# Products with V in four column groups instead of three, their lots at other slots, and a packed buffer for the small probabilities

## The chip, the cores and the metric

The kernel runs on one core of a Trainium2 chip. The metric is the device time of one execution in microseconds (us), the median of several runs. TensorE (PE) multiplies matrices, VectorE (DVE) and ScalarE (ACT) work element by element, GpSimd (POOL) and SyncE (SP) do small sums and issue transfers. PSUM is the memory into which TensorE writes, in banks of 128 partitions x 512 fp32.

## The reference, cut to what matters

32 images of 192 channels x 1024 tokens go through a channel attention (8 heads), then a token attention with a layer norm ahead, then a feed-forward part. Only the token attention is touched:

```
q = (x @ Wq).reshape(B, T, H, d)          # T = 1024, H = 6, d = 32
k, v = ...                                # the same with Wk, Wv
att = jnp.einsum('bqhd,bkhd->bhqk', q, k) * scale
att = jnp.where(causal, att, -jnp.inf)
att = jax.nn.softmax(att, axis=-1)
out = jnp.einsum('bhqk,bkhd->bqhd', att, v)
t = t + out.reshape(B, T, C)
```

Of the mask follows that query tile qt (128 queries, qt from 0 to 7) needs the keys of tiles 0 to qt alone.

## The kernel before

Five groups of six images each go through attention, and then through the feed-forward part of the group; two images are left and go through attention alone at the end. While the attention of one image runs, the "front" of the next image runs between its instructions: channel attention, layer norm, and the projections that make Q, K and V. The last image has no front beside it.

**Units and slots.** A unit is one head and one query tile: 48 per image. They are numbered n, alternate between a small tile (0 to 3) and a large one (4 to 7), and each has its slot. In slot n every engine does, in an order written out by hand:

- PE: the scores of unit n (L676, and the mask L678), once the exponential of unit n-2 has left that half of `S`; the transposes of the probabilities of unit n-3 (L690) into the two banks `PT`, up to four 128-column blocks a bank, a "chunk"; then, in some slots, a lot of products with V (L710); in some slots the transposes back of a finished batch (L719, "back" below); then a step of the next image's front (`SLOTS` gives the slot of each: xt0 to xt3, g0 to g1, wg0, wg1, na, rb, u, mt, t0 to t3, z0 to z3, qk0 to qk5, v0 to v3).
- DVE: the maximum of unit n (L1213), the copy of a large unit's first chunk to SBUF (L382), the adding of a batch to the tokens (L1199, L1201, L1207), then front work (layer norm: L1076, L1080, L1084, L1089; L1148 behind the qk steps).
- ACT: in one slot of a batch the copy of `OUT` (L925), the copy of a small unit's chunk (L928), the exponential of unit n (L936), the copy of a large unit's second chunk (L940), then front work.

Small units are turned in odd slots, large ones in even slots.

**Lots.** A lot is the product with V for three heads and one query tile. Each of its matmuls has 32 stationary columns of V and 128 moving columns, and the three heads write to partitions 0, 32 and 64 of `OUT`: three column groups of TensorE. For each key tile j the lot issues one matmul per head; this is a "step" below, and since an fp32 matmul is two instructions here, a step is six instructions. Units go in blocks of six (three heads x a small and a large tile), so an image has 16 lots and 72 steps. The small lot of block i stands in slot 6i+8, the large one in 6i+11. Four lots make a batch; ACT copies `OUT` in slot 12j+18, PE turns it back in slot 12j+19 into a `PT` bank, DVE scales and adds it.

Within an image the lots stand in slots 2, 5, 8, 11, ... 44, 47, with 3, 5, 2, 8, 4, 6, 1, 7 steps and then the same again; backs stand in slots 7, 19, 31 and 43.

**Buffers.** Turned probabilities lie in `PTS`: a ring of four per kind of unit, 512 columns each for small units and 1024 for large ones. Before it overwrites an entry, a copy waits for the lot that read it (`pv_made`). `stacked[0]` and `stacked[1]` tell that the transfers that lay out Q and K of heads 0 to 2 and 3 to 5 have landed (16 transfers per image, SP, L420).

Of the kernel before, what the change touches and what calls it, by code (L numbers as in the profile page):

```python
# [18 lines left out]
F32 = mybir.dt.float32  # L19
F16 = mybir.dt.float16  # L20
BF16 = mybir.dt.bfloat16
ALU = mybir.AluOpType
# [37 lines left out]
RING = 4  # L60
STACKS = 8 * 16
# [5 lines left out]

def qtile(n):
    return TILES[n // 6 % 4][n % 2]


def triple_of(n):
    return 2 * (n // 6) + n % 2


def unit_of(k, hh):
    return 6 * (k // 2) + k % 2 + 2 * hh


def last_slot(images):  # L80
    return 12 * (NBI * images - 1) + BACK_AT


def triples_at(images, slot):

    return [k for k in range(KI * images) if 6 * (k // 2) + PV_AT[k % 2] == slot]


def batches_at(images, slot, at):

    return [j for j in range(NBI * images) if 12 * j + at == slot]

# [9 lines left out]


def sum_col(n):

    k = triple_of(n)
    return 3 * (BATCH * (k // BATCH % SUMS) + place(k)) + n % 6 // 2

# [13 lines left out]
CHUNKS = {images: transposed(images) for images in (2, GROUP)}  # L122
PT_IMG = len(CHUNKS[2]) // 4
assert all(len(c) == 2 * PT_IMG * images for images, c in CHUNKS.items())

# [36 lines left out]
def hybrid_kernel(nc, x, wa, wb, wv, wpt, bp, temp, w3, w1, b1, w2, b2, out):  # L162
# [5 lines left out]
    with ctx:  # L168
# [3 lines left out]
        def sem(name):  # L172
# [37 lines left out]
        NK = sb("NK", [CH, 4])  # L210
        RD = sb("RD", [CH, 2, CH])
        ATT = RD
        MT = sb("MT", [CH + 1, 2, C])
# [3 lines left out]
        PROD = hi_z[0:CH + 1, :].bitcast(F32)[:, 0:4 * C].rearrange("p (a b) -> p a b", a=2)  # L217
        T0 = sb("T0", [P, 2, TT, C])
# [14 lines left out]
        T1H = T1[:, :, :, :].rearrange("p b (h t) c -> p b h (t c)", h=2)  # L233
        work = sb("work", [P, 9216])

        PS = [work[:, 0:1024].rearrange("p (a b) -> p a b", a=2), work[:, 1024:3072].rearrange("p (a b) -> p a b", a=2)]
        PTS = [work[:, 3072:5120].rearrange("p (a b) -> p a b", a=RING),
               work[:, 5120:9216].rearrange("p (a b) -> p a b", a=RING)]

# [3 lines left out]
        OT = work[:, 4096:4096 + 4 * 4 * C].rearrange("p (s n) -> p s n", s=4)  # L243
        oT = sb("oT", [CH, BATCH * P])
        rowsum = sb("rowsum", [P, 3 * BATCH * SUMS])
# [4 lines left out]
        rsums = sb("rsums", [P, 3 * BATCH])  # L250
        gm1 = sb("gm1", [P, GS, MH])
# [123 lines left out]
        def pt_copy(eng, copy, g, images, i):  # L375

            _, _, m, c0, k = CHUNKS[images][i]
            eng.wait_ge(pt_full[i % 2], after(g, 0, PT_IMG, i // 2 + 1))
            if m >= 2 * RING:

                eng.wait_ge(pv_made, after(g, 0, KI, triple_of(m - 2 * RING) + 1))
            copy(PTS[m % 2][:, m // 2 % RING, P * c0:P * (c0 + k)], PT[i % 2][:, 0:P * k]).then_inc(pt_free[i % 2], 1)  # L382

# [162 lines left out]
        def _(pe):  # L546
# [111 lines left out]
            for name in SLOTS:  # L658
                if name == "qk0":
                    pe.wait_ge(w3_ready, 1)  # L660
                front_part(name, 0, 0)

            def attention(g, images, fronts):
                for n in range(last_slot(images) + 1):
                    if n < UNITS * images:
                        u, h, qt = n // UNITS, 3 * (n % UNITS // 24) + n % 6 // 2, qtile(n)
# [13 lines left out]
                    for i, (_, kind, m, c0, k) in chunks_at(images, n):  # L680
# [4 lines left out]
                        if kind == "p":  # L685
                            if i >= 2:

                                pe.wait_ge(pt_free[i % 2], after(g, 0, PT_IMG, i // 2))
# [4 lines left out]
                    for k in triples_at(images, n):  # L693
                        u, grp, qt = k // KI, k % KI // 8, qtile(unit_of(k, 0))
                        done = [i for i, c in enumerate(CHUNKS[images]) if c[1] == "p" and c[2] <= unit_of(k, 2)]
                        for b in range(2):

                            pe.wait_ge(pt_free[b], after(g, 0, PT_IMG, max(i for i in done if i % 2 == b) // 2 + 1))
                        if k % KI == 0:

                            for step in STEPS[-2:]:
                                wait_freed(pe, g, u, step)
                        if k and k % BATCH == 0:

                            pe.wait_ge(oT_made, after(g, 0, NBI, k // BATCH))
                        o = P * place(k)
                        for j in range(qt + 1):
                            for hh in range(3):
                                h = 3 * grp + hh
                                last = mm(OUT[32 * hh:32 * hh + 32, o:o + P],  # L710
                                          V[u % 2][:, j, D * h:D * h + D], PTS[k % 2][:, unit_of(k, hh) // 2 % RING, P * j:P * j + P],
                                          start=(j == 0), stop=(j == qt), tile_position=(0, 32 * hh))
                        last.then_inc(pv_made, 1)
                    for i, (_, kind, j, _, _) in chunks_at(images, n):
                        if kind == "o":
                            pe.wait_ge(pt_free[i % 2], after(g, 0, PT_IMG, i // 2))
# [126 lines left out]
        def _(act):  # L843
# [74 lines left out]
            def attention(g, images, fronts):  # L918
                for n in range(last_slot(images) + 1):
                    for j in batches_at(images, n, OT_AT):  # L920
                        act.wait_ge(pv_made, after(g, 0, KI, BATCH * (j + 1)))
                        if j >= 1:

                            act.wait_ge(t1_step, after(g, 0, 3 * NBI, 3 * (j - 1) + 2))
                        A(oT[:, :], OUT[0:CH, :], ACT.Copy).then_inc(oT_made, 1)  # L925
                    for i, c in chunks_at(images, n):
                        if by_act(i, c) and small(c):
                            pt_copy(act, lambda o, x: A(o, x, ACT.Copy), g, images, i)  # L928
                    if n < UNITS * images:

                        act.wait_ge(max_made, after(g, 0, UNITS, n + 1))
                        if n >= 4:
                            i = max(i for i, c in enumerate(CHUNKS[images]) if c[1] == "p" and c[2] == n - 4)
                            act.wait_ge(pt_full[i % 2], after(g, 0, PT_IMG, i // 2 + 1))
                        w = P * (qtile(n) + 1)
# [69 lines left out]
        def _(dve):  # L1005
# [185 lines left out]
            def add_to_t1(g, i, j):  # L1191

                base = after(g, 0, 3 * NBI, 3 * j)
                dve.wait_ge(pt_full[i % 2], after(g, 0, PT_IMG, i // 2 + 1))
                n = 3 * BATCH
                u, grp, qts = j // NBI, j % NBI // 2, batch_tiles(j)
                ts, cols = slice(qts[0], qts[-1] + 1, 2), slice(CH * grp, CH * grp + CH)
# [3 lines left out]
                v.tensor_tensor(t1.rearrange("p t (h d) -> p t h d", h=3),  # L1201
                                PT[i % 2][:, 0:BATCH * CH].rearrange("p (t h d) -> p t h d", t=BATCH, h=3),
                                rsums[:, :].rearrange("p (t h) -> p t h", t=BATCH).unsqueeze(3).broadcast_to(
                                    [P, BATCH, 3, D]), ALU.mult).then_inc(t1_step, 1)
                dve.wait_ge(t1_step, base + 2)
# [185 lines left out]
```

## Time and profile before

| | |
|---|---|
| median of 3 runs | 4539.35 us (4538.74 to 4539.68) |
| profiled execution | 4540.19 us, its span 4538.4 us |
| PE busy | 4010.0 us (88%) |
| DVE busy | 3043.9 us (67%) |
| ACT busy | 2975.3 us (66%) |
| granted TensorE clock, mean | 0.977 |

The busy time of an engine is the union of its instructions' durations. Share of the span and bound are two things: an engine can be busy 88% of the time and yet set the pace in one stretch and wait in another. So the rows further on go by stretches of one image. A timeline row has the start, the time from the first start to the last end of the instructions merged in it, and in brackets the idle time of the engine ahead of it with what ended it.

### The profile page before, as it was taken

Reading aid. Unit: us, or ns where it says so; the run is one execution under the profiler, and the core shown is the slowest. Engines: PE = TensorE matmul, PEld = TensorE weight load, DVE = VectorE, ACT = ScalarE, POOL = GpSimd, SP = SyncE. Lnnn points to the kernel's source line nnn. Section 1 sums busy time; section 2 is a strip of 40 time slices with the busy share of each in tenths; the row PEclk is TensorE's granted clock in tenths of the full one; section 3 lists DMA queues with packets and bytes.
Section 4 is the critical chain, followed back from the end, with each engine's and each line's share of the span. In section 5 each row is a group of like instructions: output and inputs, shape, how many; then the busy total and the mean of one; then the engine's idle time right before and its main releaser. Section 6 shows DMA issues by size and latency. Waiting matters only on the chain.

```text
span 4538.4 us, 114718 instructions
## 1 busy us (share of the span) xinstructions
PE 4010.0 (88%) x39240; PEld 2939.7 (65%) x39240; DVE 3043.9 (67%) x5559; ACT 2975.3 (66%) x6669; POOL 363.7 (8%) x374
## 2 busy tenths in 40 slices
PE   6999988879999888999998879999888999898887
PEld 4767665667777646777665667777646777665665
DVE  5666666766666667666766766666666666766765
ACT  3666666657776655666676667776655676676666
POOL 1000002000000110000002000000110000002000
PEclk7999999999999999999999999999999999999999
DMA  2111111011221101111111011211101111111011
GB/s 72 37 37 36 43 36 29 1 50 36 54 47 36 36 0 43 36 37 36 43 36 29 1 50 38 57 42 36 36 0 43 37 36 41 39 36 29 1 43 43
DMA packets 48640, 161.00 MB, mean 35 GB/s; under 512 B 12420, under 2 KB 12934, under 8 KB 48006
## 3 DMA queue, kind: packets, MB, share of 16 engines
q1 hardware_dynamic: 48134, 154.39, 14.2%
q8 instruction: 300, 4.92, 0.5%
q14 instruction: 206, 1.69, 0.1%
HBM read 28.52 MB, written 25.17 MB: 12 GB/s over the span
## 4 chain that ended last, share of the span: by engine, by line
PE 63%; DVE 14%; issue 13%; ACT 6%; POOL 2%; DVEq 1%; DMA 1%; ACTq 1%; SPq 0%; POOLq 0%
PE PT L690 10%; PE OUT L710 10%; PE S L676 6%; DVE nmax L1213 5%; PE PT L808 5%; PE S L735 5%; PE S L634 3%; PE FR L634 3%; PE FR L578 2%; PE S L779 2%; ACT work L936 2%; DVE work L382 2%; DVE XT L1084 2%; PE FR L641 1%; PE S L641 1%
## 5 line engine op out<-in xcount | busy, mean ns | idle before, releaser
L1213 DVE TENSOR_REDUCE nmax<-S 128x1 f32<-128x256 f32 (+7 forms) x1536 | 1146.1, 753 | 937.0 <-PE S L678 927.0
L936 ACT ACTIVATE work<-S,nmax 128x256 f32<-128x256 f32 (+7 forms) x1536 | 1137.7, 742 | 613.9 <-DVE nmax L1213 594.8
L690 PE MATMUL PT<-ident,work 128*128 128x128 f32 x6912 | 1076.7, 280 | 93.2 <-DVE work L382 54.5
L690 PEld LDWEIGHTS PT<-ident,work 128*128 128x128 f32 x6912 | 748.2, 142 | 260.0 <-ACT work L928 54.3
L382 DVE COPY work<-PT 128x512 f32<-128x512 f32 x768 | 524.1, 682 | 45.0 <-PE PT L690 37.8
L928 ACT ACTIVATE work<-PT 128x256 f32<-128x256 f32 (+3 forms) x768 | 338.1, 440 | 153.6 <-PE PT L690 146.4
L676 PE MATMUL S<-KS,QS 128*128 128x512 f16 (+3 forms) x1152 | 323.5, 335 | 111.4 <-ACT work L936 76.9
L676 PE MATMUL S<-odd 128*128 128x512 f16 (+3 forms) x1152 | 315.5, 328 | 71.7 <-ACT work L936 68.0
L678 PE MATMUL S<-causal,identb 128*128 128x128 bf16 x1536 | 339.2, 221 | 0.0
L940 ACT ACTIVATE work<-PT 128x512 f32<-128x512 f32 (+3 forms) x768 | 332.4, 433 | 1.4 <-PE PT L690 1.4
L936 ACT ACTIVATION_READ_ACCUMULATOR work<-S,nmax 128x1 f32 x1536 | 304.6, 198 | 0.0
L735 PE MATMUL S<-odd,W1b 128*128 (+1 forms) x1080 | 259.7, 393 | 50.0 <-ACT work L979 41.7
L710 PE MATMUL OUT<-work,V 128*32 128x128 f32 x6912 | 303.1, 275 | 0.0
L710 PE MATMUL OUT<-work,odd 128*32 128x128 f32 x6912 | 302.6, 275 | 0.0
L1247 DVE TENSOR_REDUCE gm<-S 128x1024 f32 (+1 forms) x180 | 220.0, 1222 | 118.7 <-PE S L779 117.7
L779 PE MATMUL S<-odd,W1b 128*128 (+1 forms) x1080 | 291.8, 379 | 0.0
L979 ACT ACTIVATE work<-S,sc 128x512 f32<-128x512 f32 x360 | 255.0, 781 | 51.2 <-PE S L735 50.7
L710 PEld LDWEIGHTS OUT<-work,V 128*32 128x32 f32 x6912 | 234.3, 110 | 40.9 <-issue 32.3
L710 PEld LDWEIGHTS OUT<-work,odd 128*32 128x32 f32 x6912 | 234.5, 109 | 40.2 <-issue 30.7
L808 PE MATMUL PT<-W2b,work 128*128 128x192 f16 x2880 | 247.5, 246 | 8.8 <-DVE odd L1300 8.8
L808 PEld LDWEIGHTS PT<-W2b,work 128*128 128x128 f16 x2880 | 239.0, 98 | 22.9 <-DVE odd L1300 9.9
L1292 DVE SCALAR_TENSOR_TENSOR work<-work 128x1024 f16<-128x1024 f32 x180 | 218.3, 1224 | 30.2 <-ACT work L986 26.1
(208 smaller groups left out, 6113.6 us busy)
## 6 DMA issues: line engine op xcount, KB each, us to landing
X<-in_x SPq DMA_DIRECT2D x32, 768.0 KB, 5.3
odd<-hi_z SPq DMA_DIRECT2D x128, 192.0 KB, 4.2
odd<-odd SPq DMA_DIRECT2D x128, 192.0 KB, 4.3
out_y<-work SPq DMA_DIRECT2D x64, 384.0 KB, 4.0
QS<-hi_z SPq DMA_DIRECT2D x64, 192.0 KB, 3.9
QS<-odd SPq DMA_DIRECT2D x64, 192.0 KB, 4.1
KS<-hi_z SPq DMA_DIRECT2D x64, 192.0 KB, 4.6
KS<-odd SPq DMA_DIRECT2D x64, 192.0 KB, 4.7
```

Source lines behind the costliest of these rows:

```text
L382: copy(PTS[m % 2][:, m // 2 % RING, P * c0:P * (c0 + k)], PT[i % 2][:, 0:P * k]).then_inc(pt_free[i % 2], 1)
L676: mm(S[:, n % 2, c0:min(w, c0 + 512)], q, KS[u % 2][:, h, c0:min(w, c0 + 512)], start=True, stop=c0 + 512 < w)
L678: mm(S[:, n % 2, w - P:w], identb[:, :], causal[:, :], start=False, stop=True).then_inc(scores_full, 1)
L690: last = tr(bank[:, P * (j - c0):P * (j - c0) + P], PS[m % 2][:, m // 2 % 2, P * j:P * j + P], ident[:, :])
L710: last = mm(OUT[32 * hh:32 * hh + 32, o:o + P], V[u % 2][:, j, D * h:D * h + D], PTS[k % 2][:, unit_of(k, hh) // 2 % RING, P * j:P * j + P ...
L735: last = mm(bank, W1b[:, j, P * (i % 6):P * (i % 6) + P], rhs[:, j, :], start=(j == 0), stop=(j == 2))
L779: last = mm(bank, W1b[:, j, P * m:P * m + P], Z2[:, b, hf, j, :], start=False, stop=(j == 2))
L808: last = mm(PT[tp % 2][:, C * t:C * t + C], HS[:, hf, part, m, o:o + P], W2b[:, m, :], start=(m == 0 and part == 0), stop=(m == MH - 1 and ...
L928: pt_copy(act, lambda o, x: A(o, x, ACT.Copy), g, images, i)
L936: A(PS[n % 2][:, n // 2 % 2, 0:w], S[:, n % 2, 0:w], ACT.Exp, bias=nmax[:, n % MAXES:n % MAXES + 1], accum_out=rowsum[:, sum_col(n):sum_co ...
L940: pt_copy(act, lambda o, x: A(o, x, ACT.Copy), g, images, i)
L1213: v.tensor_reduce(nmax[:, n % MAXES:n % MAXES + 1], S[:, n % 2, 0:P * (qtile(n) + 1)], AX.X, ALU.max, negate=True).then_inc(max_made, 1)
```

## The change

- Units go in blocks of eight. In blocks 0 to 3 of an image these are heads 0 to 3 x (a small and a large tile); in blocks 4 and 5 they are heads 4 and 5 with two small and two large tiles each: (0, 1) and (6, 7), then (2, 3) and (4, 5).
- A lot takes four units and four column groups (`OUT` partitions 0, 32, 64, 96). An image has 12 lots. In blocks 4 and 5 a lot's two tiles differ by one, so its last step has two matmuls instead of four.
- The large lot of block i stands in slot 8i+11, the small one in slot 8i+14. Within an image: slots 3, 6, 11, 14, 19, 22, 27, 30, 35, 38, 43, 46, with 6, 4, 8, 2, 6, 4, 7, 1, 5, 3, 8, 2 steps.
- A batch is still four lots, so there are three per image, with 128 partitions and 512 columns: copied in slot 16j+23, turned back in 16j+24 (slots 8, 24, 40 of an image; the copies in 7, 23, 39).
- Turned small probabilities are packed by their width into 2304 columns, odd blocks from the end downward; turned large ones have four entries of 1024 columns. What a copy overwrites is given by `overwritten`.
- Head 3 is needed from unit 6 of an image on, so `stacked[1]` is waited for there and not at unit 24.
- `RD`, `ATT` and `MT` move into unused columns of `hi_z`, which makes room.

```
-KI = UNITS // 3
+KI = UNITS // 4
 TILES = [(1, 7), (3, 5), (0, 6), (2, 4)]
+PAIRS = [((0, 1), (6, 7)), ((2, 3), (4, 5))]
-PV_AT = (8, 11)
+PV_AT = (14, 11)
-OT_AT, BACK_AT = 18, 19
-RING = 4
+OT_AT, BACK_AT = 23, 24
+SMALL = 2304
+def head_and_tile(n):
+    block, at, large = n % UNITS // 8, n % 8 // 2, n % 2
+    if block < 4:
+        return at, TILES[block][large]
+    return 4 + at % 2, PAIRS[block - 4][large][at // 2]
+def lots_until(k):
+    return k if k % 2 else k + 2
+def turned_at(m):
+    k, hh = quad_of(m), m % 8 // 2
+    if m % 2:
+        return 1024 * hh
+    widths = [P * (qtile(unit_of(k, i)) + 1) for i in range(hh + 1)]
+    return SMALL - sum(widths) if k // 2 % 2 else sum(widths[:hh])
+def overwritten(m):
+    k = quad_of(m)
+    return k - 2 if m % 2 or m % 8 >= 4 else k - 4
...
-            if m >= 2 * RING:
-                eng.wait_ge(pv_made, after(g, 0, KI, triple_of(m - 2 * RING) + 1))
+            if overwritten(m) >= 0:
+                eng.wait_ge(pv_made, after(g, 0, KI, lots_until(overwritten(m))))
...
+                for j in range(max(qtile(m) for m in units) + 1):
+                    for hh, m in enumerate(units):
+                        h, qt = head_and_tile(m)
+                        if j <= qt:
+                            last = mm(OUT[32 * hh:32 * hh + 32, o:o + P], V[u % 2][:, j, D * h:D * h + D],
+                                      PTS[k % 2][:, turned_at(m) + P * j:turned_at(m) + P * j + P],
+                                      start=(j == 0), stop=(j == qt), tile_position=(0, 32 * hh))
...
-                        if n % 24 == 0:
-                            pe.wait_ge(stacked[n % UNITS // 24], after(g, u, STACKS, STACKS))
+                        if n % UNITS in (0, 6):
+                            pe.wait_ge(stacked[h // 3], after(g, u, STACKS, STACKS))
...
-                                last = tr(PT[i % 2][:, CH * q:CH * q + CH], oT[:, P * q:P * q + P],
-                                          ident[0:CH, 0:CH])
+                                last = tr(PT[i % 2][:, P * q:P * q + P], oT[:, P * q:P * q + P], ident[:, :])
```

## Rows read from the trace of the kernel before

**Rows 1.** The page: engines' busy time, and its chain that ended last.

```profile
PE 4010.0 (88%) x39240; PEld 2939.7 (65%) x39240; DVE 3043.9 (67%) x5559; ACT 2975.3 (66%) x6669; POOL 363.7 (8%) x374
...
PE 63%; DVE 14%; issue 13%; ACT 6%; POOL 2%; DVEq 1%; DMA 1%; ACTq 1%; SPq 0%; POOLq 0%
```

**Rows 2.** Busy time by window: one whole image, then the image without a front.

```profile
core 0: us, PE busy (x) PEld busy (x) DVE busy (x) ACT busy (x) POOL busy (x), PEclk, DMA share, GB/s
...
1147.20:1250.00 102.80, 94.69 (x1021) 72.54 (x1020) 69.12 (x132) 72.12 (x179) 6.03 (x5) 1.00 0.17 40
...
4440.10:4517.20 77.10, 64.15 (x740) 45.59 (x738) 54.06 (x84) 55.40 (x145) 0.00 (x0) 1.00 0.05 12
```

**Rows 3.** Busy time by window: slots 0-11, 12-23, 24-34, 35-47 of that image.

```profile
1146.80:1173.90 27.10, 26.45 (x283) 21.06 (x281) 15.47 (x23) 18.18 (x45) 0.00 (x0) 1.00 0.14 33
1173.90:1199.80 25.90, 22.98 (x242) 18.88 (x241) 17.08 (x42) 16.22 (x45) 1.00 (x1) 1.00 0.01 2
1199.80:1220.00 20.20, 16.29 (x170) 11.26 (x167) 18.40 (x38) 14.74 (x35) 5.03 (x4) 1.00 0.16 40
1220.00:1249.60 29.60, 28.99 (x332) 21.32 (x332) 18.17 (x28) 22.98 (x55) 0.00 (x0) 1.00 0.37 80
```

**Rows 4.** PE's timeline, slots 35 and 43 to 44: lots of 8 and of 1 step, a back.

```profile
1220.41 0.60 PE L690 MATMUL PT<-ident,work 128*128 128x128 f32 x4
1220.95 1.95 PE L710 MATMUL OUT<-work,V 128*32 128x128 f32 x48
1222.83 0.39 PE L634 MATMUL FR<-zt,W3h 128*128 128x512 f16 x1
...
1241.09 0.50 PE L719 MATMUL PT<-ident,oT 96*128 96x96 f32 x4
1241.42 0.25 PE L641 MATMUL FR<-W3h,zt 128*128 128x192 f16 x1
...
1243.49 0.42 PE L710 MATMUL OUT<-work,V 128*32 128x128 f32 x6
1243.85 0.26 PE L641 MATMUL S<-W3h,zt 128*128 128x192 f16 x1
```

**Rows 5.** PE's timeline, slots 2 to 5.

```profile
1150.01 0.86 PE L710 MATMUL OUT<-work,odd 128*32 128x128 f32 x18
...
1154.41 0.60 PE L676 MATMUL S<-KS,QS 128*128 128x512 f16 x2 [0.65 <-ACT work L936]
```

**Rows 6.** Timeline, slots 17 to 19: the wait of front step u, the back.

```profile
1181.26 0.55 PE L676 MATMUL S<-KS,QS 128*128 128x512 f16 x2 [0.99 <-ACT work L936]
...
1181.91 1.51 PE L710 MATMUL OUT<-work,V 128*32 128x128 f32 x36
...
1185.78 0.89 PE L610 MATMUL FR<-WPT,RD 96*96 96x192 f32 x4 [1.26 <-DVE RD L1129]
...
1187.40 0.54 PE L719 MATMUL PT<-ident,oT 96*128 96x96 f32 x4 [0.23 <-ACT work L940]
```

**Rows 7.** DVE's timeline, slots 24 to 31: only first rows and the batch.

```profile
1200.18 0.42 DVE L1213 TENSOR_REDUCE nmax<-S 128x1 f32<-128x256 f32 x1 [2.23 <-PE S L678]
1200.71 0.69 DVE L382 COPY work<-PT 128x512 f32<-128x512 f32 x1
1201.32 1.21 DVE L1213 TENSOR_REDUCE nmax<-S 128x1 f32<-128x1024 f32 x1
...
1214.46 0.23 DVE L1199 RECIPROCAL rsums<-rowsum 128x12 f32<-128x12 f32 x1 [0.56 <-PE PT L719]
1214.72 0.56 DVE L1201 TENSOR_TENSOR T<-PT,rsums 128x384 f32<-128x384 f32 x1
1215.44 0.56 DVE L1207 TENSOR_TENSOR T<-T 128x384 f32<-128x384 f32 x1 [0.16 <-DVE T L1201]
```

**Rows 8.** PE's timeline at the end of a group's attention.

```profile
718.67 2.11 PE L710 MATMUL OUT<-work,odd 128*32 128x128 f32 x48
```

**Rows 9.** SP's timeline: the last stacking transfers of the image.

```profile
1249.61 2.06 SPq L420 DMA_DIRECT2D odd<-odd  x2
```

More of the change, by code:

```diff
@@ L65, with quad_of, quads_at @@
          284: "next_stats1", 285: "next_aggregate", 286: "turn0", 287: "turn1", 288: "turn2", 289: "turn3"}
-def qtile(n):
-    return TILES[n // 6 % 4][n % 2]
-def triple_of(n):
-    return 2 * (n // 6) + n % 2
+def head_and_tile(n):
[3 more added lines that the diff above has]
+    return 4 + at % 2, PAIRS[block - 4][large][at // 2]
+def qtile(n):
+    return head_and_tile(n)[1]
+def quad_of(n):
+    return 2 * (n // 8) + n % 2
+def lots_until(k):
+    return k if k % 2 else k + 2
 def unit_of(k, hh):
-    return 6 * (k // 2) + k % 2 + 2 * hh
+    return 8 * (k // 2) + k % 2 + 2 * hh
 def last_slot(images):
-    return 12 * (NBI * images - 1) + BACK_AT
-def triples_at(images, slot):
-    return [k for k in range(KI * images) if 6 * (k // 2) + PV_AT[k % 2] == slot]
+    return 16 * (NBI * images - 1) + BACK_AT
+def quads_at(images, slot):
+    return [k for k in range(KI * images) if 8 * (k // 2) + PV_AT[k % 2] == slot]
 def batches_at(images, slot, at):
-    return [j for j in range(NBI * images) if 12 * j + at == slot]
+    return [j for j in range(NBI * images) if 16 * j + at == slot]
 def batch_tiles(j):
@@ L122 @@
 CHUNKS = {images: transposed(images) for images in (2, GROUP)}
-PT_IMG = len(CHUNKS[2]) // 4
-assert all(len(c) == 2 * PT_IMG * images for images, c in CHUNKS.items())
+PT_GROUP = len(CHUNKS[GROUP]) // 2
+assert len(CHUNKS[GROUP]) == 2 * PT_GROUP
 STEPS = ["xt0", "xt1", "xt2", "xt3", "g0", "g1", "wg0", "wg1", "na", "rb", "u", "mt", "t0", "t1", "t2", "t3",
@@ L661, in _, with times_v @@
                 front_part(name, 0, 0)
+            def times_v(g, images, k):
+                u, units = k // KI, [unit_of(k, hh) for hh in range(4)]
+                done = [i for i, c in enumerate(CHUNKS[images]) if c[1] == "p" and c[2] <= units[3]]
+                for b in range(2):
+                    pe.wait_ge(pt_free[b], g * PT_GROUP + (max(i for i in done if i % 2 == b) // 2 + 1))
+                if k % KI == 1:
+                    for step in STEPS[-2:]:
+                        wait_freed(pe, g, u, step)
+                if k > BATCH and k % BATCH == 1:
+                    pe.wait_ge(oT_made, after(g, 0, NBI, k // BATCH))
+                o = P * place(k)
+                for j in range(max(qtile(m) for m in units) + 1):
[5 more added lines that the diff above has]
+                                      start=(j == 0), stop=(j == qt), tile_position=(0, 32 * hh))
+                last.then_inc(pv_made, 1)
             def attention(g, images, fronts):
@@ L686, in attention @@
                             if i >= 2:
[L688 removed]
+                                pe.wait_ge(pt_free[i % 2], g * PT_GROUP + i // 2)
                             for j in range(c0, c0 + k):
@@ L692, in attention @@
                             last.then_inc(pt_full[i % 2], 1)
[L693 to L713, printed above, removed]
+                    for k in quads_at(images, n):
+                        times_v(g, images, k)
                     for i, (_, kind, j, _, _) in chunks_at(images, n):
                         if kind == "o":
-                            pe.wait_ge(pt_free[i % 2], after(g, 0, PT_IMG, i // 2))
+                            pe.wait_ge(pt_free[i % 2], g * PT_GROUP + i // 2)
                             pe.wait_ge(oT_made, after(g, 0, NBI, j + 1))
                             for q in range(BATCH):
-                                last = tr(PT[i % 2][:, CH * q:CH * q + CH], oT[:, P * q:P * q + P],
-                                          ident[0:CH, 0:CH])
+                                last = tr(PT[i % 2][:, P * q:P * q + P], oT[:, P * q:P * q + P], ident[:, :])
                             last.then_inc(pt_full[i % 2], 1)
@@ L1193, in add_to_t1 @@
                 base = after(g, 0, 3 * NBI, 3 * j)
[L1194 to L1197, printed above, removed]
+                dve.wait_ge(pt_full[i % 2], g * PT_GROUP + (i // 2 + 1))
+                n = 4 * BATCH
+                u, qts = j // NBI, batch_tiles(j)
+                if j % NBI < 2:
+                    ts, cols, nt, nh = slice(qts[0], qts[-1] + 1, 2), slice(0, 4 * D), 4, 4
+                else:
+                    ts, cols, nt, nh = slice(0, TT), slice(4 * D, C), TT, 2
                 t1 = T1[:, u, ts, cols]
```

43 lines of the change are left out of this document (22 added, 21 removed).

## The prediction

> **What bounds the kernel now.** I read the page first. TensorE is busy 88% of the span, VectorE 67%, ScalarE 66%, and 63% of the chain that ended last is PE's [rows 1]. That says where to look, not what a PE microsecond is worth, because attention is a loop across three engines: scores, maximum, exponential, and the scores two units later. So I next took windows. An image with a front takes 102.8 us with PE busy 94.69; the image without one takes 77.1 us with PE busy 64.15 [rows 2]. The front adds 30.5 us of PE work and 25.7 us of time, so PE is nearly the bound, but with 8.1 us of idle time that is not spread evenly.
>
> Windows by stretch of slots show where it is [rows 3]. In slots 0 to 11 PE is busy 26.45 of 27.10 us and in slots 35 to 47 28.99 of 29.60: what leaves PE there leaves the time. In slots 12 to 23 it idles 2.9 us. In slots 24 to 34 it is busy only 16.29 of 20.20 us, while DVE, which does the layer norm there, is busy 18.40: DVE sets that stretch. The change has to be priced stretch by stretch.
>
> **Price of a lot.** A lot of 8 steps (48 instructions) occupies PE from its start to the start of the next work for 1222.83 - 1220.95 = 1.88 us, a lot of one step for 0.36 us [rows 4]. A step is then (1.88 - 0.36) / 7 = 0.217 us, whatever the number of heads in it as far as three go, and a lot costs 0.14 us more behind it. Four transposes ahead of the long lot last 0.54 us, of which about 0.44 is theirs (0.109 each, the pitch of half a step), so 0.10 is the change into the lot [rows 4]. I take 0.24 us per lot beside its steps.
>
> The step has three heads in three column groups before and four in four after. No row shows four side by side. If the fourth fits, a step stays 0.217 us. If it does not, the bound is one third more, 0.29 us. I take 0.217: with three heads 1.52 us for 42 instructions are 36 ns for each, while the transposes ahead, which also stream 128 fp32 columns but use all columns of the array, come at about three times that (0.54 us for four, the change included). So the three groups do run side by side, at the pitch of one. The skill's page "TensorE: Matmul & The Clock Gate", Part 3 on packing small matmuls, gives 2.38x for three column tiles and 3.07x for four row tiles. By that ratio four heads would take 1.034 times the step of three, an estimate of 0.4 us more per image on 56 steps; no run here shows it yet, and the sum below does without it.
>
> **PE's work, per image.** Steps fall from 72 to 56: 16 x 0.217 = 3.47 us. Lots fall from 16 to 12: 4 x 0.24 = 0.96 us. A back costs 1241.42 - 1241.09 = 0.33 us at 96 rows [rows 4]; at 128 a third more, 0.44; four at 0.33 against three at 0.44 is nothing. The ceiling is thus 4.43 us per image. Now by stretch, with what hides or exposes each.
>
> **Slots 0 to 11.** 18 steps before and after, one lot fewer: -0.24. One back before and after: +0.11. The lot in slot 2 is in a part where the exponential sets the pace; without it PE waits there for the same exponential and gains little, while the lot now in slot 3 fills the 0.65 us that PE idled ahead of slot 5 [rows 5]. About +0.05. The back now stands in an even slot, behind a large unit's two chunks; its bank is the one of the first chunk, which DVE frees only after its maximum: in slot 24 that copy ends 1201.40 - 1199.82 = 1.6 us into the slot [rows 7], and PE has turned its eight blocks by about 1.2. A wait of 0 to 0.65 us, taken as 0.4. Sum +0.3 us.
>
> **Slots 12 to 23.** 18 steps become 12 (-1.30), four lots three (-0.24), and the back leaves (-0.33): -1.87. But the lot in slot 17 runs while front step u waits for the channel softmax (DVE and ACT); PE idles 1.26 us more after it [rows 6]. That chain hangs on the scores of unit 17, not on the lot, so without the lot PE waits its 36 instructions' time longer: +1.54. The 0.23 us of waiting ahead of the back [rows 6] goes. Sum -0.56 us.
>
> **Slots 24 to 34.** Three lots become two, but PE is not the bound, so that is worth nothing by itself. DVE adds one batch in the stretch before (slot 31) and one after (slot 24). Before, DVE idled 0.56 us for the transposes and worked 1.35 us [rows 7]. After, the tensors have 512 columns instead of 384, an estimate of 1.6 us, and stand between the maximum of unit 24 and that of unit 25: maximum 25 started 1.5 us into slot 24 and would start at about 3.9, 2.4 us later, and the layer norm is queued behind it; the exponential of unit 25 and the scores of unit 27 wait for it. At slot 31 1.35 + 0.56 = 1.9 us come back. In sum +0.4 if DVE has no slack; -1.1 if the removal at slot 31 relieves PE and ACT too and the delay at slot 24 is absorbed by the idle time that DVE has ahead of it (2.23 us [rows 7]). The middle, -0.35.
>
> **Slots 35 to 47.** 26 steps become 18 (-1.74), five lots four (-0.24), the back +0.11, its wait in slot 40 +0.4. With the long lot gone from slot 47, PE reaches the next image's scores before the exponential of unit 47 has ended: +0.35, an estimate. Sum -1.1 us.
>
> **Other parts.** A large lot now waits for chunks turned one slot earlier (slot 8i+10, copied by ACT behind the exponential), three slots before. Where a front step lies between them that is hidden; in slots 3 and 27 it may cost up to 0.5 us each, inside the bounds above. The small lot stands five slots behind its last transposes and waits for nothing. The packed buffer is overwritten only after lots that PE has already issued: nothing. `stacked[1]` is now needed 18 units sooner; the last transfers are issued by 1251.67 [rows 9], slot 6 starts about 11 us after 1249.61, so with a few us to land it is in time. Moving `MT` and its like costs no instruction.
>
> **End of a group.** The last two lots run there back to back, 8 steps in 2.11 us [rows 8]; after, they have 10 and the long one, which waits for the last copies, comes first: +1.0 us, at five groups and the end, +6 us.
>
> **Sum.** 0.3 - 0.56 - 0.35 - 1.1 = -1.7 us per image; 31 images have a front: -53 us. The image without one is paced by the three-engine loop: 0. With the +6: -47 us on the profiled 4540.2 us, 4493 us; the median lies 0.8 us below the profiled run, so 4492 us.
>
> **Rivals.**
> - *PE's whole saving shows* (chance 0.15). The waits merely shift. For it: PE is 92% busy. Against it: the 18.40 us of DVE [rows 3] and the 1.26 us [rows 6]. 31 x 4.43 = 137 us: 4402 us.
> - *It evens out* (0.12). Stretch two gains nothing as its waits grow by all that leaves, stretch three takes +0.4, the two bank waits are 0.65: +0.55 + 0 + 0.4 - 0.85 = +0.1 per image, 31 x 0.1 + 6 us, 4548 us.
> - *DVE's batch at slot 24 is not recovered* (0.13), the one on the other side. If the 2.4 us by which maximum 25 slips reach the end of the stretch, because slots 31 to 34 are set by ACT's copies and not by the batch that left, stretch three costs +2.3 instead of -0.35: 31 x 2.65 = 82 us more, 4574 us. It turns the sign once it costs 47 / 31 = 1.5 us per image more than in my sum. Against it: PE and DVE both lose work at slot 31.
> - *The fourth group does not fit* (0.05). A step of 0.29 us: 40 of 56 steps lie on the path, 31 x 40 x 0.073 = 91 us more, 4583 us. The row's 36 ns per instruction speaks against it.
> The forecast holds 0.55, with its own range 4450 to 4525.
>
> **How the numbers follow.** Within 0.2% is 4530 to 4548, about what a measurement can tell from no change. Faster takes the forecast and the first rival, 0.70; the even case gives 0.13 with the edges of its neighbours, slower 0.17. The range that leaves out 2 in 10 cuts most of the slower rivals and the far end of the first: 4422 to 4550 us.
>
> **What would show it.** Per step 0.217 us with 8 instructions; windows of one image with PE busy about 90.3 us and a length near 101; PE waiting longer ahead of front step u; a wait for DVE's copy ahead of the backs in slots 8, 24 and 40; maximum 25 late by 2 us. The prediction is wrong if a step grows, if large lots wait for ACT's second chunk in most blocks, or if slots 24 to 34 get longer.

## The result, and the profile after

The changed kernel takes 4732.4 us (4726.0 to 4738.9, 4 runs) against 4539.5 us before, a ratio of 1.043 [1.041, 1.044]: 193 us slower, where 47 us faster was forecast with a range up to 4550.

The page of the kernel after, engines' busy time:

```profile
PE 3993.5 (84%) x39057; PEld 2924.3 (62%) x39112; DVE 3070.5 (65%) x5463; ACT 2941.6 (62%) x6637; POOL 362.8 (8%) x374
```

TensorE's busy time fell by only 16.5 us [rows 1]; four fewer lots and 16 fewer steps per image should take 31 x 4.43 = 137 us from it, and the image without a front another 4. So something else on TensorE got longer. The granted clock tells what: its mean is 0.949 after and 0.977 before. The clock has two levels, 2.4 and 1.2 GHz, so the half level held for (1 - 0.949) x 2 x 4729 = 482 us after and 209 us before.

Busy time by window after, the same image and the same stretches as in [rows 3]: slots 0 to 11, 12 to 23, 24 to 34, 35 to 47. The column ahead of the last two is the granted clock:

```profile
1193.40:1221.90 28.50, 26.86 (x312) 21.68 (x313) 16.50 (x24) 19.92 (x48) 0.00 (x0) 1.00 0.17 39
1221.90:1248.90 27.00, 23.30 (x228) 18.65 (x226) 16.68 (x39) 15.76 (x44) 1.00 (x1) 0.94 0.01 2
1248.90:1272.80 23.90, 16.72 (x168) 12.15 (x167) 17.66 (x38) 13.44 (x36) 5.01 (x4) 0.86 0.14 34
1272.80:1303.50 30.70, 28.18 (x314) 20.00 (x315) 19.28 (x28) 21.95 (x53) 0.00 (x0) 1.00 0.31 71
```

Against [rows 3] all four are longer: +1.4, +1.1, +3.7 and +1.1 us, together 110.1 us for 102.8. The two stretches in the middle are no longer at full clock; before, in this image, all four were. The image shown is one of the longer ones. Over 20 images (the second to the fifth of each group of six) the mean is 109.5 us for 103.1, and the four stretches take 1.3, 0.9, 3.0 and 1.1 us more; a table at the end of the experiments has these means for every run. The half clock of the two middle stretches is in all 31 images that have a front.

TensorE's timeline after, slots 11, then 18 and 19:

```profile
1217.88 1.96 PE L711 MATMUL OUT<-work,V 128*32 128x128 f32 x64
1219.76 1.52 PE L625 MATMUL FR<-ones,hi_z 97*96 97x1 f32 x16
...
1229.81 1.18 PE L743 MATMUL PT<-ident,work 128*128 128x128 f32 x6
1233.68 0.89 PE L640 MATMUL FR<-WPT,hi_z 96*96 96x192 f32 x4 [2.70 <-DVE hi_z L1162]
...
1235.21 2.79 PE L711 MATMUL OUT<-work,V 128*32 128x128 f32 x48
1237.93 1.67 PE L645 MATMUL S<-zt,WV 96*97 96x192 f32 x8
```

Two things are to be read here. The lot of 8 steps with four heads, 64 instructions, occupies TensorE for 1219.76 - 1217.88 = 1.88 us, to the hundredth what the lot of 8 steps with three heads took [rows 4]. The fourth column group is free. And the lot of six steps in slot 19, 48 instructions, takes 2.72 us to the next start, where 6 x 0.217 + 0.14 = 1.44 us are its price at full clock. Ahead of it TensorE had idled for 2.70 us at front step u. The idle time itself was in the sum (1.26 us before, 1.54 more); what it did to the clock was not.

Windows of TensorE after: the wait in slot 18, slot 19, slot 27.

```profile
1229.70:1233.60 3.90, 1.15 (x10) 0.68 (x7) 1.93 (x6) 2.41 (x7) 0.00 (x0) 1.00 0.01 2
1234.40:1239.40 5.00, 5.00 (x62) 4.00 (x60) 1.11 (x2) 2.06 (x5) 0.00 (x0) 0.66 0.01 3
1254.80:1260.40 5.60, 4.48 (x63) 3.25 (x64) 3.43 (x12) 2.32 (x6) 1.84 (x2) 0.54 0.00 0
```

In slot 19 TensorE is busy all of the time at a mean clock of 0.66. In slot 27 it is 0.54. Why TensorE came to wait ahead of slot 27 stands in two timelines after, slots 24 to 27. VectorE:

```profile
1249.74 0.68 DVE L412 COPY work<-PT 128x512 f32<-128x512 f32 x1
1251.24 0.25 DVE L1235 RECIPROCAL rsums<-rowsum 128x16 f32<-128x16 f32 x1 [0.82 <-PE PT L753]
1251.53 0.69 DVE L1237 TENSOR_TENSOR T<-PT,rsums 128x512 f32<-128x512 f32 x1
1252.37 0.69 DVE L1243 TENSOR_TENSOR T<-T 128x512 f32<-128x512 f32 x1 [0.15 <-DVE T L1237]
1252.98 0.82 DVE L1249 TENSOR_REDUCE nmax<-S 128x1 f32<-128x640 f32 x1
```

TensorE:

```profile
1250.55 0.65 PE L753 MATMUL PT<-ident,oT 128*128 128x128 f32 x4 [0.55 <-DVE work L412]
...
1254.77 0.44 PE L729 MATMUL S<-KS,QS 128*128 128x512 f16 x2 [1.40 <-ACT work L969]
...
1256.39 0.88 PE L743 MATMUL PT<-ident,work 128*128 128x128 f32 x3 [1.12 <-ACT work L969]
1257.20 3.21 PE L711 MATMUL OUT<-work,V 128*32 128x128 f32 x56
```

The batch of slot 24 waits for the copy of the large unit's first chunk (0.55 us on TensorE), then for the back (0.82 us on VectorE), then takes 1.7 us; only then comes the maximum of unit 25 (L1249, at 1252.98), 4.1 us into slot 24. Before it was 1.5 us [rows 7]. The exponential and with it the scores of unit 27 come late, TensorE idles 1.40 and 1.12 us, and the long lot runs at half clock: 3.15 us to the next start for 7 x 0.217 + 0.14 = 1.66.

In slot 40 the back waits in the same way, and a little later front step v0:

```profile
1287.87 0.65 PE L753 MATMUL PT<-ident,oT 128*128 128x128 f32 x4 [0.82 <-DVE work L412]
...
1291.15 0.26 PE L671 MATMUL FR<-W3h,zt 128*128 128x192 f16 x1 [0.79 <-DVEq L1185]
```

### The profile page after: what moved, and what is told of

Same layout as the page of the kernel before. It is cut to its first block, busy times and chain, and to the rows that moved or that the text cites. A ratio compares the mean times of both kernels' runs of the same rounds, so it can differ in the third digit from the quotient of the medians.

```text
span 4729.1 us, 114023 instructions
## 1 busy us (share of the span) xinstructions
PE 3993.5 (84%) x39057; PEld 2924.3 (62%) x39112; DVE 3070.5 (65%) x5463; ACT 2941.6 (62%) x6637; POOL 362.8 (8%) x374
## 4 chain that ended last, share of the span: by engine, by line
PE 60%; DVE 14%; issue 14%; ACT 7%; POOL 2%; DMA 1%; DVEq 1%; ACTq 1%; SPq 1%; POOLq 0%
PE OUT L711 10%; PE PT L743 10%; PE S L729 6%; PE PT L841 5%; PE S L768 4%; DVE nmax L1249 4%; DVE work L412 2%; ACT work L969 2%; PE S L812 2%; PE FR L608 2%; PE S L664 2%; PE FR L664 2%; PE FR L671 1%; PE PT L753 1%; PE S L731 1%
## 5 line engine op out<-in xcount | busy, mean ns | idle before, releaser
L1249 DVE TENSOR_REDUCE nmax<-S 128x1 f32<-128x256 f32 (+7 forms) x1536 | 1146.0, 753 | 964.3 <-PE S L731 932.1
L743 PE MATMUL PT<-ident,work 128*128 128x128 f32 x6912 | 1096.4, 284 | 140.2 <-DVE work L412 50.2
L743 PEld LDWEIGHTS PT<-ident,work 128*128 128x128 f32 x6912 | 769.0, 145 | 298.9 <-ACT work L961 59.8
L961 ACT ACTIVATE work<-PT 128x256 f32<-128x256 f32 (+3 forms) x768 | 339.2, 442 | 157.6 <-PE PT L743 148.6
L711 PE MATMUL OUT<-work,V 128*32 128x128 f32 x6912 | 271.1, 304 | 12.5 <-ACT work L973 12.5
L711 PE MATMUL OUT<-work,odd 128*32 128x128 f32 x6912 | 254.8, 292 | 14.5 <-ACT work L973 14.5
L711 PEld LDWEIGHTS OUT<-work,V 128*32 128x32 f32 x6912 | 211.3, 122 | 51.0 <-issue 30.9
L731 PEld LDWEIGHTS S<-causal,identb 128*128 128x128 bf16 x1536 | 154.2, 100 | 128.8 <-issue 21.0
```

The source lines that it names most:

```text
L711: last = mm(OUT[32 * hh:32 * hh + 32, o:o + P], V[u % 2][:, j, D * h:D * h + D], PTS[k % 2][:, turned_at(m) + P * j:turned_at(m) + P * j + P],
L1249: v.tensor_reduce(nmax[:, n % MAXES:n % MAXES + 1], S[:, n % 2, 0:P * (qtile(n) + 1)], AX.X, ALU.max, negate=True).then_inc(max_made, 1)
```

## The experiments

Two causes were to be told apart: theory C (the clock falls after TensorE's longer waits, and that is time lost) and theory D (the batch stands in the wrong slots for VectorE, and the clock only follows where TensorE waits anyway). Unless it says otherwise, each kernel is the changed kernel with the edit shown. "Image" is the length of the four stretches of one image in its profile; the kernel before has 27.1, 25.9, 20.2, 29.6 us there, the changed one 28.5, 27.0, 23.9, 30.7. The ratio behind each time is to the kernel before, run alongside.

**e1, matmuls in the waits.** Their results are not used; all other work is unchanged.

```
+                    for _ in range(7):       # front step u, ahead of its wait
+                        mm(FR[0:CH, 0:C], WPT[:, 0, 0:CH], WPT[:, 1, :], start=True, stop=True)
                     pe.wait_ge(xsoft, after(g, u, XSOFT, XSOFT))
...
+                    if n % UNITS in {26: 4, 30: 4} and n // UNITS < fronts:
+                        keep_busy(g, n // UNITS + 1, {26: 4, 30: 4}[n % UNITS])
```

> The changed kernel with extra matmuls that no result uses, in places where TensorE only waits: 7 ahead of front step u's wait (slot 18), 4 at the end of slots 26 and 30 of an image. The extra outputs are overwritten by the step's own. Theory C (the clock): TensorE idles about 2.7 us in slot 18 and 3.6 us in slots 24 to 27, its granted clock falls to half for 6.8 to 10.2 us per image, and that costs half of this time, 3.4 to 5 us per image, 100 to 150 us in all. It expects 4580 to 4640 us, no stretch of an image at half clock, and the lot in slot 19 back from 2.8 to about 1.5 us. Theory D (the order of DVE's work alone makes the loss, and the clock only follows without a price, since TensorE waits there anyway) expects 4715 to 4735 us: the extra matmuls hide in waits and give nothing back.

Measured: 4626.5 us, 1.020 [1.018, 1.021]: 106 us less than the changed kernel, by adding work. TensorE's timeline in slots 18 and 19:

```profile
1201.13 2.44 PE L639 MATMUL FR<-WPT 96*96 96x192 f32 x14
1203.99 0.89 PE L642 MATMUL FR<-WPT,hi_z 96*96 96x192 f32 x4 [0.42 <-DVE hi_z L1171]
...
1205.36 1.52 PE L713 MATMUL OUT<-work,V 128*32 128x128 f32 x48
```

and its windows, the two middle stretches:

```profile
1192.20:1217.60 25.40, 23.97 (x242) 19.69 (x241) 16.69 (x39) 15.72 (x44) 1.00 (x1) 1.00 0.01 2
1217.60:1239.10 21.50, 16.87 (x184) 12.82 (x183) 17.65 (x38) 13.51 (x36) 5.02 (x4) 1.00 0.15 39
```

Step u comes as late as before, but the lot behind it takes 1.52 us for 2.79. The clock is full in both stretches, in all 31 images. They lose 1.6 and 2.4 us against the changed kernel in the image shown, 1.7 and 1.8 us on the mean of 20 images, while the outer two stay (28.4 and 30.8 on the mean). 31 x 3.4 us is the whole gain. Theory C holds, with 106 of the 193 us; theory D alone does not explain the result.

**e9, the control.** The same kind of edit in the kernel before (4 matmuls ahead of u, 3 in slots 26 and 30).

> The kernel before with matmuls that no result uses, 4 ahead of front step u's wait and 3 at the end of slots 26 and 30. The control of the clock theory: the kernel before keeps the full clock there (a half clock shows at the start of a group alone), so theory C expects no gain, 4537 to 4560 us. If these matmuls gave time for another reason (the weights' queue, the order of the loads), the kernel before would gain too: under 4525 us.

Measured: 4543.1 us, 1.0007 [0.9998, 1.0016]. What was expected about the kernel before is not quite so: its clock falls not at the start of a group alone, but also in slots 12 to 23 of five of the 31 images, behind the same wait at front step u as in the others. One of the five, its stretch and its wait:

```profile
1379.54:1407.07 27.53, 24.61 (x242) 20.02 (x241) 17.09 (x42) 16.21 (x45) 1.00 (x1) 0.94 0.01 2
...
1391.35 0.89 PE L610 MATMUL FR<-WPT,RD 96*96 96x192 f32 x4 [1.26 <-DVE RD L1129]
```

That makes the control sharper. With the matmuls no image of e9 has half clock in slots 12 to 23, and all take 25.9 us: the five get 1.7 us each back, the others get nothing. In slots 24 to 34, where the clock was full but for the first images of groups, the matmuls cost 0.6 us per image (20.8 for 20.2). So they give time only where the clock had fallen, and it is the clock that e1 got back. Since they cost time of their own, 106 us is, if anything, too little for it.

**e2, the backs in slots 15, 31 and 47.**

```
-OT_AT, BACK_AT = 23, 24
+OT_AT, BACK_AT = 23, 31
```

> The changed kernel with the batches turned back and added in slots 15, 31 and 47 of an image (16j+31) instead of 8, 24 and 40; the copy of OUT stays in slot 16j+23. Theory D: the batch's three DVE instructions (about 1.8 us with their wait) no longer stand ahead of the maximum of unit 25 and of the layer norm, nor behind a large unit's copy; slots 24 to 34 shorten from 23.9 to about 20.5 us, slots 0 to 11 and 35 to 47 by about 1 us each: 4560 to 4600 us, with the clock still falling at slot 19 alone. Theory C alone (the clock falls for lack of lots in slots 17 and 26): slots 24 to 34 still hold a stretch at half clock, 4690 to 4735 us.

Measured: 4638.5 us, 1.022 [1.020, 1.024], 94 us less than the changed kernel. Its windows:

```profile
1164.10:1192.70 28.60, 26.77 (x310) 21.20 (x308) 16.25 (x24) 19.57 (x48) 0.00 (x0) 1.00 0.16 36
1192.70:1221.80 29.10, 24.68 (x232) 19.44 (x230) 18.14 (x42) 15.89 (x44) 1.00 (x1) 0.88 0.01 1
1221.80:1241.60 19.80, 14.28 (x167) 10.33 (x165) 17.66 (x38) 13.35 (x36) 5.02 (x4) 1.00 0.17 41
1241.60:1270.10 28.50, 27.72 (x314) 20.17 (x315) 17.89 (x26) 22.16 (x53) 0.00 (x0) 1.00 0.35 79
```

The time lies between what the two theories expected. Slots 24 to 34 fall from 23.9 to 19.8 us and slots 35 to 47 from 30.7 to 28.5, both now shorter than before the change in this image; on the mean of 20 images slots 24 to 34 take 20.2 us, as before the change, since the clock still falls there in 21 of 31 images. But a batch now stands in slot 15, in the chain of the channel softmax: the wait ahead of u grows to 3.0 us, the stretch to 29.1 us and its clock falls to 0.88. In slots 0 to 11 nothing is gained, against what was expected. Slot 8, which the back left, does get 1.2 us shorter (and slot 9 0.7 longer), but the batch of slot 47 now stands ahead of the maximum of unit 0, which starts only 1.9 us into the next image:

```profile
1165.39 0.69 DVE L1243 TENSOR_TENSOR T<-T 128x512 f32<-128x512 f32 x1 [0.15 <-DVE T L1237]
...
1166.00 0.42 DVE L1249 TENSOR_REDUCE nmax<-S 128x1 f32<-128x256 f32 x1
```

**e3, the backs one slot later.** `OT_AT, BACK_AT = 23, 25`.

> The changed kernel with the batches turned back one slot later, in the odd slots 9, 25 and 41. There the bank that the back takes was freed a slot earlier by ACT, so TensorE does not wait for DVE's copy (0.6 to 0.8 us each, three per image), but the batch still stands in the stretch of the layer norm, now behind the maximum of unit 25. If the wait for the bank is what matters: about 2 us per image, 4665 us. If the place in the layer norm matters: nearly all of the loss of slots 24 to 34 stays, 4690 to 4720 us.

Measured: 4691.1 us, 1.033 [1.032, 1.035]; image 27.8, 25.4, 23.9, 29.4 us. One slot later gives 41 us, 0.9 us per image of it in slots 35 to 47 and 0.3 in slots 0 to 11, where the wait for the bank is shorter (29 us over the run for 60, all releasers together). The full clock in slots 12 to 23 of the profiled image is not the rule: 8 of 31 images have it, with the same wait of 2.70 us at step u as the others, and the mean of that stretch falls by 0.2 us only. Slots 24 to 34 stay at 23.9 us with a clock of 0.86: there it is the batch's place in front of the layer norm that costs, not the bank.

**e4, the small lots in slot 8i+10.** One of four steps then stands in slot 18, ahead of step u, and one in slot 26.

```
-PV_AT = (14, 11)
+PV_AT = (10, 11)
...
-    return k if k % 2 else k + 2
+    return k + 1
```

> The changed kernel with the small lots in slot 8i+10 instead of 8i+14, so that a lot of four steps stands in slot 18 ahead of front step u, and one in slot 26; the large lots stay. Theory C: TensorE idles 1.1 us less in slot 18, perhaps enough to keep the clock up in slot 19; and the lot is hidden in a wait instead of standing on the path in slot 22: 1 us per image by itself, 2.5 to 3 us if the clock stays up there. 4640 to 4700 us. Theory D expects only the hidden lot: 4700 us.

Measured: 4631.7 us, 1.021 [1.019, 1.023], 101 us less than the changed kernel. TensorE's timeline, slots 18 and 19:

```profile
1205.58 1.08 PE L711 MATMUL OUT<-work,V 128*32 128x128 f32 x32
1208.34 0.89 PE L640 MATMUL FR<-WPT,hi_z 96*96 96x192 f32 x4 [1.68 <-DVE hi_z L1162]
...
1209.71 1.52 PE L711 MATMUL OUT<-work,V 128*32 128x128 f32 x48
```

The lot takes its own time out of the wait, 2.70 to 1.68 us, and the lot of slot 19 is back at full clock. Slots 12 to 23 take 24.2 us for 27.0: 1.0 us from the lot that is now hidden and most of the rest from the clock (1.7 us in e1), which is full here in 26 of 31 images. A lot of two steps also moved from slot 14 to slot 10, into the stretch before. In slots 24 to 34 nothing changes (23.9 us, clock 0.86), and slots 35 to 47 are 0.7 us shorter. The time is somewhat below the range of theory C and far below that of theory D.

**e5, both: small lots in 8i+10 and backs in 15, 31, 47.**

> The changed kernel with small lots in slot 8i+10 (so one in slot 18 and one in slot 26) and the backs in slots 15, 31 and 47. The two edits alone gave -101 and -94 us. If they mend two different places, they add: stretch by stretch the better of the two gives about 28.5 + 25 + 20.2 + 28.5 = 102.3 us per image against 103.5 before, 4500 to 4545 us. If both gave only the clock back, they do not add: 4610 to 4630 us.

Measured: 4566.0 us, 1.006 [1.005, 1.008]. The two edits together gave 166 us where the sum of the two is 195; image 28.6, 25.8, 21.0, 27.9. They add for the most part; the time lies between the two expected ranges. What is missing lies in the two middle stretches, 26.5 and 20.7 us on the mean of 20 images where 25 and 20.2 were expected. The image shown has full clock in slots 12 to 23, but 17 of 31 images do not, and in slots 24 to 34 its clock is 0.92.

**e6, the same with unused matmuls** (4 ahead of u, 3 at the end of slots 26 and 30).

> The run with small lots in slot 8i+10 and backs in slots 15, 31, 47, with matmuls that no result uses: 4 ahead of front step u's wait, 3 at the end of slots 26 and 30. If some clock is still lost there (slot 19's lot at half clock), it comes back: 20 to 60 us below the same kernel without them. If the lots now in slots 18 and 26 keep the clock up already: within 10 us of it.

Measured: 4521.9 us, 0.9964 [0.995, 0.998]: 44 us less than e5, and the first kernel that is faster than the one before, by 0.4%. Its windows:

```profile
1137.50:1166.10 28.60, 27.26 (x325) 21.59 (x324) 16.31 (x24) 19.77 (x48) 0.00 (x0) 1.00 0.13 32
1166.10:1191.90 25.80, 23.35 (x225) 18.90 (x224) 18.09 (x42) 15.88 (x44) 1.00 (x1) 1.00 0.01 2
1191.90:1212.10 20.20, 16.94 (x203) 12.70 (x202) 17.83 (x38) 13.84 (x36) 5.02 (x4) 1.00 0.15 41
1212.10:1239.90 27.80, 26.95 (x294) 19.59 (x292) 17.81 (x25) 21.78 (x53) 0.00 (x0) 1.00 0.38 82
```

The gain over the kernel before is in the last stretch, 27.8 for 29.6 us; the first is 1.5 us longer.

**e12, the same with the small lots where the change has them** (8i+14; 7 matmuls ahead of u, 4 in slots 26 and 30).

> The changed kernel with the backs in slots 15, 31 and 47 and the unused matmuls (7 ahead of u, 4 in slots 26 and 30), the small lots where the change has them (8i+14). Against the same with small lots in 8i+10 (4522 us) it tells what the small lots' place costs with the clock kept up. If the place only cost the clock: 4515 to 4530 us. If the lot of four steps in slot 22 stands on the path while slot 18 has a wait free for it: about 1.1 us per image more, 4550 to 4570 us.

Measured: 4557.7 us, 1.004 [1.003, 1.006], 36 us above e6: with the clock kept up, the place of the small lots costs 1.2 us per image. Slots 12 to 23 are 26.9 for 25.8 us. (The two kernels also differ in the number of unused matmuls, 15 and 10 per image; on the mean, slots 35 to 47 are 0.8 us longer and slots 24 to 34 0.5 us shorter.)

The same run answers another question. Against e1 only the place of the backs differs, and both have full clock in the middle stretches: 4626.5 against 4557.7 us. So the place of the batches costs 69 us, 2.2 us per image, that are not the clock's. Theories C and D both hold, one beside the other.

**e7, small lots in 8i+10 and backs in 13, 29 and 45.**

> As the run with small lots in slot 8i+10 and backs in 31, but with the backs in slots 13, 29 and 45 (16j+29). In slot 15 the batch stood in the channel softmax chain and slots 12 to 23 took 1.5 us more than with the back in slot 8. In slot 13 it is ahead of that chain, but in slot 29 DVE still has the rounding of the layer norm: slots 12 to 23 a microsecond shorter, slots 24 to 34 one to two longer, 4510 to 4570 us.

Measured: 4601.3 us, 1.015 [1.013, 1.016], above the expected range. Image 27.9, 27.6, 21.2, 29.2: slots 12 to 23 did not get shorter, their clock is 0.94, and slots 35 to 47 are 1.3 us longer than with the backs in 31 and 47.

**e8, the large lots in 8i+12, ahead of the slot's transposes,** with the rest as in e5.

> As the run with small lots in slot 8i+10 and backs in 31, but the large lots one slot later, in 8i+12, ahead of the transposes of that slot instead of behind them. It takes away the wait of the large lot for ACT's copy of the second chunk (27 us in the changed kernel in all). If that wait is what keeps slots 0 to 11 a microsecond longer than before: 20 to 30 us faster. If the lot ahead of the transposes makes DVE's copies late instead: no gain or slower by up to 30 us.

Measured: 4622.7 us, 1.018 [1.017, 1.020], 57 us above e5, twice the loss that was allowed for. Image 27.0, 29.3, 21.0, 28.6. Slots 0 to 11 are 1.6 us shorter, but that is no gain: the lot of eight steps, 1.88 us, left slot 11 for slot 12 and is now counted in the next stretch. Slots 12 to 23 are 3.5 us longer, 1.9 of it that lot. On the median of 20 images the slot starts lie 0.4 us behind e5's at slot 13, 1.1 at slot 21 and 2.2 at slot 37. Behind the transposes in 8i+11 is the better place of the two; that VectorE's copies come late is the expectation's reason, and was not isolated.

**e10, the channel softmax one slot sooner,** with the rest as in e5 and no unused matmuls.

```
-SMALL_SLOTS = {..., "logits": 16, "xexp": 17, "attn": 17.5,
+SMALL_SLOTS = {..., "logits": 16, "xexp": 16, "attn": 16.5,
```

> The run with small lots in slot 8i+10 and backs in 15, 31, 47, without unused matmuls, and with the channel softmax one slot sooner: its exponential (xexp) behind unit 16's and its scaling (attn) ahead of the maximum of unit 17. It shortens TensorE's wait ahead of front step u by a real cause. If that wait (some 4 us in slots 17 and 18) is what lets the clock fall in slot 19: 1 to 1.5 us per image and the clock besides, 4490 to 4535 us against 4566. If the maximum of unit 17 is then what comes last, the wait moves and nothing is gained: 4555 to 4575 us.

Measured: 4535.2 us, 0.9989 [0.998, 0.9998], 31 us below e5 and just outside the expected range. TensorE no longer waits at step u (2.0 us in e5), but part of the wait has moved: ahead of the transposes of slot 18 it now waits 1.4 us per image for ACT's copy (L961), for 0.1 in e5. The clock falls in slots 12 to 23 of 5 images of 31, for 17 in e5; in slots 24 to 34 it is still 0.92.

**e11, e10 with unused matmuls in slots 26 and 30 alone.**

> As the run with the softmax one slot sooner, with 3 matmuls that no result uses at the end of slots 26 and 30. If the clock still falls in the layer norm's stretch without them, 15 to 40 us below it: 4470 to 4510 us, the fastest of all. If it does not fall there: the same time.

Measured: 4522.8 us, 0.9964 [0.995, 0.998], no better than e6. The 12 us below e10 are less than expected; in the profiled image slots 12 to 23 show a clock of 0.94 (26.5 us, e10 25.3), and so do 13 of the 31 images, for 5 in e10. The clock came back in one stretch and fell in another, in which the kernel is the same; why is open.

**All runs side by side.** Means over 20 images (the second to the fifth of each group) in us, from the start of a slot's scores on TensorE to the next, and the number of images, of 31, whose clock is not full in the stretch. The four images counted for slots 24 to 34 before are first images of groups.

| | 0 to 11 | 12 to 23 | 24 to 34 | 35 to 47 | image | not full, 12 to 23 | not full, 24 to 34 |
|---|---|---|---|---|---|---|---|
| before | 27.1 | 26.2 | 20.2 | 29.6 | 103.1 | 5 | 4 |
| after | 28.5 | 27.1 | 23.2 | 30.7 | 109.5 | 31 | 31 |
| e1 | 28.4 | 25.4 | 21.4 | 30.8 | 106.1 | 0 | 0 |
| e9 (before) | 27.1 | 25.9 | 20.8 | 29.6 | 103.4 | 0 | 0 |
| e2 | 28.7 | 29.1 | 20.2 | 28.6 | 106.5 | 31 | 21 |
| e3 | 28.1 | 26.9 | 23.5 | 29.8 | 108.2 | 23 | 31 |
| e4 | 28.4 | 24.3 | 23.3 | 30.0 | 106.0 | 5 | 31 |
| e5 | 28.6 | 26.5 | 20.7 | 28.1 | 103.9 | 17 | 30 |
| e6 | 28.6 | 25.7 | 20.2 | 27.8 | 102.4 | 0 | 4 |
| e12 | 28.7 | 26.9 | 19.7 | 28.6 | 103.9 | 0 | 0 |
| e7 | 28.1 | 26.9 | 21.2 | 29.1 | 105.4 | 15 | 28 |
| e8 | 27.0 | 29.3 | 21.0 | 28.7 | 106.0 | 29 | 30 |
| e10 | 28.6 | 25.4 | 20.9 | 28.1 | 103.1 | 5 | 28 |
| e11 | 28.6 | 26.0 | 20.3 | 27.8 | 102.7 | 13 | 8 |


## Why the prediction was wrong

**How far off, and where.** On the mean of 20 images an image took 6.4 us more, where 1.7 less was forecast: 8.1 us apart. The clock is 3.4 of them (e1). The other 4.7 are in e1's stretches at full clock: slots 0 to 11 +1.3 us for +0.3, slots 12 to 23 about as forecast, slots 24 to 34 +1.2 for -0.35, slots 35 to 47 +1.2 for -1.1. Two steps failed outright, and slots 0 to 11 were priced too low. The prediction had named slots 24 to 34 getting longer as a sign that it is wrong, and they did.

**The first step that failed** is the one in slots 12 to 23: "without the lot PE waits its 36 instructions' time longer: +1.54". The wait was sized rightly. It came out as 2.70 us, and 1.26 + 1.54 is 2.80. The mistake was to price it as idle time and nothing else. After it the clock was at half, and the lot behind it took nearly twice its time. With the clock kept up (e1) the stretch is 25.4 us, 0.5 less than in an image of before at full clock, where -0.56 was forecast. The same happened in slots 24 to 34 behind other waits. In all the clock made 106 us of the 193 (e1, with e9 as control). The Trainium skill's page "TensorE: Matmul & The Clock Gate", section "HAM oscillation", describes this pattern in a loop that waits for a DMA: after each wait the next piece of work starts on the slow clock. The trace after agrees in kind, with 0.66 in slot 19 and 0.54 in slot 27; the waits here are for other engines, and shorter than those of the page's example. None of the rivals had it.

**The second step that failed: the batch in slots 8, 24 and 40**, priced at -0.35 us in slots 24 to 34 ("the middle") and at 0.11 + 0.4 us in each of the other two stretches. The rival "DVE's batch at slot 24 is not recovered" had the mechanism, but not the size: it let the whole slip reach the end of the stretch. The maximum of unit 25 slipped from 1.5 to 4.1 us into slot 24; 2.4 us of slip were forecast. At full clock 1.3 us of it stayed (21.5 us in e1 for 20.2), where the sum took a gain of 0.35; with the clock it was 3.7 us in the image shown, 3.0 on the mean. The wait for the bank came out at 0.57, 0.55 and 0.82 us in slots 8, 24 and 40, taken as 0.4 with 0.65 as its bound. What the sum left out was who waits behind the batch in slot 40, front step v0 (0.79 us). Slots 35 to 47 lost 1.1 us where 1.1 us of gain was forecast; these two waits (0.82 and 0.79 us, of which the sum had 0.4) make 1.2 of the 2.2 us between, and the rest was not traced to a wait. But with the backs moved (e2) all 2.2 us are gone: 28.5 us. Moving the backs gave 94 us in all, and 69 us with the clock kept up on both sides (e12 against e1).

**Slots 0 to 11** came out at +1.4 us for +0.3. The slot starts show where. Slot 6 starts 11.0 us into the image before and after, although two steps fewer lie ahead of it: what left TensorE in slots 0 to 5 did not leave the time, against "what leaves PE there leaves the time". From slot 6 to slot 9 it is 8.1 us for 6.8, with two steps more (0.43 us), the longer back (0.11) and the wait for the bank (0.57). The large lot in slot 3 waits for ACT's chunk (0.22 us in the image shown; all lots together 27 us over the run), which was in the bounds. (The slot starts are medians of 20 images.) No run isolates these terms: e2, whose total for the stretch stays at 28.6, gains in slot 8 and loses in slots 0 to 2.

**What was right.** The fourth group is free: 1.88 us for 64 instructions as for 48, so the rival in which it does not fit falls, and so does the estimate of 1.034 for a step from the packing figures of the Trainium skill's page "TensorE: Matmul & The Clock Gate", Part 3: the measurement decides. Slots 12 to 23 at full clock came out as the sum had them. That slots 35 to 47 with the backs moved gain 1.0 us is near the sum's -1.1 by luck: without a back there the sum would be -1.6. `stacked[1]` was in time: the scores' waits for transfers sum to 9 us over the run, 7 before. The end of a group was priced somewhat too high, at +1.0 us. TensorE's timeline after has the last two lots in one piece, 2.39 us for 2.11 [rows 8], behind a wait of 0.54 us that the lots before did not have:

```profile
753.86 2.39 PE L711 MATMUL OUT<-work,odd 128*32 128x128 f32 x72 [0.54 <-ACT work L973]
```

That is 0.8 us; from the last scores to the end of the last back it is 10.1 us for 9.5.

The saving of TensorE's work is real, but in no kernel here was it worth its 4.4 us per image: the best has 102.4 us per image on the mean, for 103.1.

## What to carry to other kernels

When work leaves a place where an engine waits, the wait grows by what leaves; on TensorE ask also whether the clock will hold over it, and price the work behind it at half clock if not. Spare lots belong into the longest known wait, not at an even pitch (36 us here, e6 against e12). A time read for a stretch of slots is no gain if the edit moved work over the stretch's edge (e8), and one image is not the kernel: count in how many images the clock falls. A batch that another engine has to finish is placed by that engine's queue: look at what stands behind it there in every one of its slots, not at the slot where it costs least to issue.

## What the runs showed of the hardware

In these runs the wait at front step u is nearly the same in every image of a kernel, and what the clock does behind it is not. It was below full in slots 18 to 20 of these numbers of images, of 31:

| kernel | wait at step u, median us | images |
|---|---|---|
| before | 1.26 | 5 |
| e4 | 1.69 | 5 |
| e5 | 2.0 | 17 |
| after | 2.70 | 31 |
| e3 | 2.70 | 23 |
| e2 | 3.1 | 31 |

With a longer wait the fall is seen more often, but the same 1.26 us left the clock full in 26 images and did not in 5, and the same 2.70 us left it full in 8 images of e3. In e10 TensorE does not wait at step u at all, and the clock still falls there in 5 images. So a single wait's length does not decide it in these traces. Two waits half a microsecond apart, 1.40 and 1.12 us, were followed by half clock too (after, slots 26 and 27). Adding 15 matmuls per image whose results nobody reads made a kernel 106 us faster.
